# TensorE's loop over tiles: eight bodies a round in place of one

## The reference, cut to what matters

```python
xz = xh @ in_proj_w; xc, z = split(xz, 2)          # 192 channels each
xc = silu(depthwise_conv3x3(xc) + conv_b)
xs = stack([x0, x1, x0[::-1], x1[::-1]])           # rows, columns, both reversed
dts, Bs, Cs = split(xs projected by x_proj_w)      # 6, 16 and 16 rows
delta = softplus(dt_w @ dts + dt_b)
h = h * exp(delta * A) + (delta * u) * B           # 64 steps, 16 states a channel
y = sum over the states of h * C, + D * u
y = layernorm(y of the four directions) * silu(z)
out = x + alpha * (h + y @ out_proj_w)
```

## Time and profile before

| | |
|---|---|
| median of 3 runs | 32911.3 us (32894.19 to 32969.46) |
| profiled execution | 33004.65 us |
| its span, first to last instruction | 33003.0 us |
| mean granted TensorE clock | 0.978 of full speed |
| TensorE, VectorE, GpSimd, ScalarE busy | 91%, 84%, 78%, 71% |

### The profile page before, as it was taken

The page is one execution under the profiler, slowest core; times in us unless marked ns, Lnnn a source line. Parts: engine busy times, 40 slices in busy tenths (PEclk is TensorE's granted clock), DMA queues, the critical chain, the costliest instruction groups (busy, mean ns, idle before and its releaser), DMA issues.

```text
span 33003.0 us, 1064758 instructions
## 1 busy us (share of the span) xinstructions
PE 30120.5 (91%) x437486; PEld 11514.8 (35%) x437486; DVE 27835.3 (84%) x18447; ACT 23550.4 (71%) x37239; POOL 25868.9 (78%) x13288
## 2 busy tenths in 40 slices
PE   8999899999999999999999999999999999999998
PEld 2333333333333333333333333333333333333333
DVE  7888788888888888888888888888888888888888
ACT  4555677777777777777777777777777777777777
POOL 0000788888888888888888888888888888888888
PEclk9999999999999999999999999999999999999999
DMA  3333444444444444444444444444444444444444
GB/s 87 83 83 75 89 93 95 93 96 93 94 93 95 92 96 93 94 95 94 95 93 95 93 95 91 96 93 95 92 96 93 94 95 93 96 93 95 94 95 87
DMA packets 3822553, 3054.56 MB, mean 93 GB/s; under 512 B 2184848, under 2 KB 2987792, under 8 KB 3796944
## 3 DMA queue, kind: packets, MB, share of 16 engines
q1 hardware_dynamic: 3809888, 2910.77, 42.5%
q0 software_dynamic: 8560, 77.41, 0.6%
HBM read 2325.71 MB, written 449.58 MB: 84 GB/s over the span
## 4 chain that ended last, share of the span: by engine, by line
PE 27%; POOL 25%; issue 25%; ACT 6%; DVE 5%; DMA 1%; POOLq 0%; SPq 0%; ACTq 0%; DVEq 0%
POOL state L940 21%; PE dbu L1030 9%; PE pp L1127 5%; PE yb L1052 4%; DVE state L1468 3%; POOL dd L947 3%; PE pp L1121 2%; PE pp L1101 2%; POOL dd L960 1%; PE pp L1149 1%; PE pp L1090 1%; DVE dg L1458 1%; ACT state L1252 1%; DVE yf L1483 1%; ACT sp_a L1319 1%
## 5 line engine op out<-in xcount | busy, mean ns | idle before, releaser
L1468 DVE TENSOR_TENSOR_SCAN state<-state,dbu 128x1024 f32<-128x1024 f32 x9408 | 21163.6, 2275 | 4211.5 <-PE dbu L1030 4101.8
L940 POOL TENSOR_TENSOR state<-state,cc 128x1024 f32<-128x1024 f32 x9408 | 22050.9, 2370 | 3371.1 <-DVE state L1468 3367.0
L1252 ACT ACTIVATE state<-dl,a_neg 128x512 f32<-128x512 f32 x18816 | 12208.6, 711 | 21.3 <-PE yb L1052 3.2
L1030 PE MATMUL dbu<-dg,du_t 64*32 64x256 f32 x301056 | 10603.8, 390 | 1440.4 <-DVE state L1468 758.1
L1030 PEld LDWEIGHTS dbu<-dg,du_t 64*32 64x32 f32 x301056 | 4833.8, 107 | 7978.7 <-issue 6915.7
L1052 PE MATMUL yb<-state,mask 128*32 128x256 f32 x75264 | 6230.5, 396 | 145.5 <-issue 68.1
L1458 DVE TENSOR_TENSOR dg<-b_t,mask_q 128x1024 f32<-128x1024 f32 x3136 | 3756.6, 1198 | 41.6 <-PE b_t L1069 41.6
L1052 PEld LDWEIGHTS yb<-state,mask 128*32 128x32 f32 x75264 | 1515.9, 108 | 4233.6 <-issue 3598.7
L229 POOL DMA_DIRECT2D act_d<-acted x32 | 16.2, 507 | 3208.7 <-DVE mixed L489 2903.5
L1333 ACT ACTIVATE sp_y<-pp 128x512 f32<-128x512 f32 x1176 | 702.6, 597 | 1832.7 <-PE pp L1127 1832.7
L1121 PE MATMUL pp<-xd,dt_l 128*128 128x512 f32 x2352 | 1387.2, 673 | 465.7 <-DVE yf L1483 463.0
(11 more groups left out here) (170 smaller groups left out, 26428.9 us busy)
## 6 DMA issues: line engine op xcount, KB each, us to landing
dl<-dlx SPq DMA_DIRECT2D x4704, 256.0 KB, 4.9
cc<-cd SPq DMA_DIRECT2D x3136, 256.0 KB, 6.2
dlx<-dd SPq DMA_DIRECT2D x1176, 256.0 KB, 2.0
shifted<-in_x SPq DMA_DIRECT2D x384, 392.0 KB, 12.6
xs<-ye SPq DMA_DIRECT2D x1176, 112.0 KB, 2.9
xs<-ye SPq DMA_DIRECT2D x588, 128.0 KB, 2.9
image<-in_x SPq DMA_DIRECT2D x32, 1176.0 KB, 24.5
act_d<-acted POOLq DMA_DIRECT2D x32, 1176.0 KB, 9.3
```

The source lines that it names most:

```text
L940: nc.gpsimd.tensor_tensor(its, its, cc[:, h, s, :], ALU.mult).then_inc(hc_done, 1)
L1030: last = nc.tensor.matmul(dst[:, :, TQ * e:TQ * e + TQ], du_t[its, j, col:col + JC], dg[its, h, 2 * k + s, MG * TQ * g:MG * TQ * g + MG * ...
L1252: nc.scalar.activation(state[:, slot, :, m * WPX:m * WPX + WPX].rearrange("p (q k) t -> p q k t", k=2), by_place(dl[:, J // 2, 2 * h + J % ...
L1468: nc.vector.tensor_tensor_scan(its, its, dbu[p % 2][:], 0.0, ALU.mult, ALU.add).then_inc(scan_done, 1)
```

## The change

TensorE's loop in `layer1` holds `body` eight times, with b = i * 8 + 1 + turn in round i. NT - 2 = 194 tiles make 24 rounds; the two tiles that are left over, 193 and 194, are written out straight behind the loop. The loops of the other engines stay.

```diff
 AHEAD, LAG = 4, 5
+TURNS = 8
...
                 body(-1)
                 body(0)
-                with pe.Fori(1, NT - 1, 1) as b:
+                rounds = (NT - 2) // TURNS
+                if rounds > 1:
+                    with pe.Fori(0, rounds, 1) as i:
+                        for turn in range(TURNS):
+                            body(i * TURNS + 1 + turn)
+                for b in range(1 + (rounds * TURNS if rounds > 1 else 0), NT - 1):
                     body(b)
                 body(NT - 1)
                 body(NT)
```

## The result

The changed kernel takes 32627.3 us (median of 4 runs, 32618.3 to 32636.7) against 32907.6 us: a ratio of 0.991, 95% interval 0.989 to 0.993 (4 runs of it too, one more than in the table above). It is faster, by 280 us, where 714 us were forecast and 32010 to 32420 us was the range. The profiled execution of the changed kernel took 32626.6 us, that of the kernel before 33004.65 us; between the two traces lie 378 us.

The account below looks back on a forecast made before the run. No engine alone was taken to bound the kernel; TensorE's stop at each taken branch stops the others. 170 x 4.20 = 714 us off the 33003.0 us span gives 32290, from the median 32197 us; range 32010 to 32420.

Parts of the forecast that it names:

- What the branch is: TensorE's layer 1 loop line: a taken branch, median 5.466 us, must first fetch its target outside the two pages held.
- The count: TensorE's layer 1 loop: 193 taken branches become 23, so 170 are removed.
- 4.20 us a branch: Tile 1, entered without a taken branch, takes 146.59 us against 150.79 for the others: 4.20 us saved per removed branch.
- Does it hold for eight tiles in a row?: Straight tiles: VectorE's 128.6 and GpSimd's 131.6 us of work fit in 146.6 us, leaving room for the whole gain.
- absorbed: Straight tiles: VectorE or GpSimd falls behind and becomes the bound; half the gain lost, 357 us, 32554; chance 0.07.
- slower: Eight bodies' straight code is fetched late, idling TensorE inside tiles; at 0.40 us a piece 394 us slower, 33305; chance 0.03.
- Register work: TensorE's wait values from i * 8 + 1 + turn: extra instructions hidden, taken as 0; uncovered, 286 us in all.
- Profile and median: Whole run: the runs' median lies 93 us below the profiled execution, so the saving taken from it gives 32197 us.
- 632 us: Unprofiled saving over the removed branches if all 93 us between profile and median lay in the 193 branches.
- The signs of being wrong: Turns inside a round over 148 us, new "issue" waits inside tiles, or remaining branches beyond 8 us.

Follow-up runs that it names:

- e9: Changed kernel with a tile's eight output stores ahead of the next tile's first-phase delta transfer on SyncE's queue: 32304.7 us, 0.979.
- e10: Kernel before the change, with the eight output stores ahead of the next tile's first-phase delta transfer on SyncE's queue: 32783.6 us, 0.993.
- e1: Changed kernel with the first-phase C rows of half 1 fetched for tile 0 alone, output not the reference's: 32311.6 us, 0.983.
- e6: Kernel before the change, with the four small C stores of phase 1 behind the last delta transfer and half 1's C rows: 32948.3 us, 1.000.
- e2: Kernel before the change, with the first-phase C rows of half 1 fetched for tile 0 alone: 32894.7 us, 1.001.

## Why the prediction was right and wrong, step by step

- **What the branch is.** Right. 5.1 us each, TensorE's alone, shorter with a hint. The instruction queue moved 3630 pieces for 3998: 368 / 170 = 2.2 pieces of 16.4 KB less for each branch that is gone. That agrees with the Trainium skill (Runtime: NRT & Kernel Launch, Instruction fetch mechanics), by which a taken branch out of the pages held breaks the prefetch. The 108 ns that the Trainium skill gives for a compare-and-branch (Advanced Engine Details and Errata, Control Flow Timing) does not hold for a body of this length.
- **The count.** Right: 170 fewer taken branches.
- **4.20 us a branch.** The step that failed, in the sentence "The trace before holds a direct sample". Tile 1 is not a sample of the other straight tiles: it is the only one in the loop without another tile's output stores ahead of it on SyncE's queue. The 4.20 us held the branch and the stores together, and the stores stayed. One removed branch measured 2.27 us between the traces, and the straight tiles were 1.94 us longer than tile 1 because GpSimd's step 4 waited for C rows that came late. With the stores out of the way straight tiles take 146.87 us (e9), and the sample nearly works: in e10, the same order with one body a round, tile 1 takes 146.56 us and a tile behind a branch 149.60, 3.04 us more, and the change brought 479 us there, 2.82 us a branch. That 33011.3 - 32304.7 = 707 us is so near to the 714 of the prediction is luck: 228 us of it are the order's own.
- **The shortfall, added up.** 714 - 280 = 434 us: 714 - 386 = 328 us are the straight tiles, 386 - 378 = 8 us the rest between the traces, and 378 - 280 = 98 us lie between the profiled executions and the medians.
- **"Does it hold for eight tiles in a row?"** Wrong, and the place where it could have been seen. It compared the busy time of VectorE and GpSimd with 146.6 us and never asked the transfers. The trace of before had it: in the looped tiles the C rows landed at 17.2 us and step 4 began at 19.2, with 2.0 us to spare, while tile 1's pace needs step 4 at 14.6, 4.6 us earlier. The rows would have had to land 2.6 us earlier for that; without the branch they landed 1.7 us earlier (15.5). The first of these numbers could be read before, the second could not.
- **The rival "absorbed".** Its time, 32554, was near the result, its chance of 0.07 far too low, its mechanism wrong: VectorE and GpSimd kept up, as e1 and e9 show.
- **The rival "slower", late code.** A small part of it is true. In 97 of the 170 straight tiles a new block of code begins in the crowded stretch (read from where the stops lie: in the second, fourth, sixth and eighth body of a round and in tile 194), and in 75 of these TensorE stops in the midst of `inputs`; in the 73 others it never does. One such stop, in TensorE's timeline:

```profile
4348.70 1.07 PE L1031 MATMUL dbu<-dg,du_t 64*32 64x256 f32 x25
4351.09 0.63 PE L1031 MATMUL dbu<-dg,du_t 64*32 64x256 f32 x7 [1.32 <-issue]
```

  There are 75 such stops, 108.6 of the 144.9 us of "issue" at `dbu` (most stops at the branches are put down to other waits). They aren't added to the rest: the 97 tiles take 148.06 us, the 73 without such a block 149.13. In the 97 the C rows of half 1 were issued at 5.0 us on average, in the 73 at 6.0; why the two kinds differ in this was not tried. In e1, which has less traffic, the stops are gone, and in e9 38 are left, 19.7 us in all.
- **Register work.** Right, it costs nothing here: a straight tile of the changed kernel has 113 register instructions on TensorE's sequencer, a looped one of the kernel before 120, so the eight bodies add none, and e9's straight tiles stand within 0.3 us of tile 1's 146.6. It wasn't tried alone.
- **Profile and median.** The profiled execution of before was 97 us above its median, that of after at its median. So 378 us between traces are 280 us between medians. The prediction had seen this: its 632 us take it in, and the result is outside the range even so.
- **The signs of being wrong.** Two of the three that the prediction gave came up: turns inside a round are longer than 148 us (148.52), and new "issue" waits stand inside the tiles. The "issue" at `dbu` is 144.9 us and not 92, and VectorE's wait for `dbu` fell by 286 us (4101.8 to 3815.6) and not by 500.

## What to carry to other kernels

When a stall goes, ask of everything that was waiting with it when it would have been ready, the transfers first: the slack of each against its use is in the trace of before. A tile at the edge of a loop is a fine sample of one thing only if its queues hold the same work as all the others; compare the DMA queue's list before its time is multiplied. And where transfers are the new limit, the order of the queue can be worth more than the change that showed it: here eight stores, issued ahead of a wait that they had no part in, gave 382 us.

## What the hardware showed that I had not expected

- A taken branch to a far target isn't of fixed length: the stop it makes went from 3.9 to 2.8 us when output stores left that stretch (e10), with 228 us in the median. Part of such a difference between traces can be that of two executions: it is 3.4 us in e6 and 3.2 us in e2, and neither is faster than the kernel before. It ended some 1.4 us behind the end of a 16 KB packet of the instruction queue.
- Straight code can be late too, where transfers crowd: up to 2.7 us in the midst of a run of matmuls, 75 times in the changed kernel, 38 times with the stores moved (e9), and never in e1, with 1 MB less a tile.
- The same prefetch hint left 4.19 us of branch in a loop of one body and 0.45 and 2.24 us in loops of eight (medians).
